# A loads-and-sums move: W_out fetched and its column sums taken in the SSM stage, and the second head pair's weight copy placed behind the first half-unit's copies

## The reference, cut to what matters

```python
xn = layernorm(x)
s = L0_attn(xn)          # 16 heads of 128, elu(q)+1 and elu(k)+1, causal linear attention, @ Wo.T
g = silu(L0_ffn(xn))     # 8 experts, top 2, and a shared one
x = x + s * g
xn = layernorm(x)
zxbca = xn @ W_in.T      # L1_attn: x, z, b, c of 32 heads x 64, and a
decay = exp(-exp(a))
states = states * decay + x_t * b_t      # a scan over 1024 tokens, per head a 64x64 state
y = (states @ c_t + x_t * D) * silu(z)
y = (y - mean(y)) * rsqrt(var(y) + 1e-5) * gamma + beta    # over 2048
s = y @ W_out.T
g = silu(L1_ffn(xn))     # int weights: (wq - 128) * scale; gate, up, down, 704 wide
x = x + s * g
```

## Time and profile before

| | |
|---|---|
| times of three executions | 1805.13, 1802.15, 1801.72 us; median 1802.15 |
| the profiled execution | 1803.97 us |
| its span, first to last instruction | 1802.2 us |
| mean granted TensorE clock | 0.969 |
| busy: TensorE, DVE, ACT, POOL | 92%, 64%, 42%, 37% of the span |
| last phase of batch 0 and of batch 1 begins at | 432.9 us, 1334.1 us |
| first SSM projection of the two batches | 504.1 us, 1399.5 us |

### The profile page before, as it was taken

How to read it: one execution, slowest core, us unless ns; L and a number is a source line. 1 busy time by engine, 2 the same in 40 slices (tenths; PEclk the granted TensorE clock), 3 DMA queues, 4 the chain that set the end, 5 groups by cost and what they waited for, 6 DMA issues and landing times.

```text
span 1802.2 us, 29615 instructions
## 1 busy us (share of the span) xinstructions
PE 1652.1 (92%) x11068; PEld 1370.2 (76%) x11068; DVE 1153.2 (64%) x2041; ACT 758.6 (42%) x1379; POOL 664.2 (37%) x500
## 2 busy tenths in 40 slices
PE   5997899898979999999969978998989899999988
PEld 3886677796868888887938866777968788888878
DVE  4334788653857777777753347886535677777767
ACT  3333455333434444444534334553334344444445
POOL 1454444101114555444514534441012155444535
PEclk9999999999989999999979989999999999999999
DMA  2333000001224443441023320000012343343410
GB/s 76 103 103 117 18 36 1 1 1 56 71 85 127 126 133 118 129 140 49 13 70 103 108 111 19 36 1 1 1 56 71 96 139 118 122 140 126 132 33 25
DMA packets 60061, 135.68 MB, mean 75 GB/s; under 512 B 8128, under 2 KB 12736, under 8 KB 59408
## 3 DMA queue, kind: packets, MB, share of 16 engines
q1 hardware_dynamic: 59920, 133.79, 23.6%
HBM read 130.81 MB, written 2.95 MB: 74 GB/s over the span
## 4 chain that ended last, share of the span: by engine, by line
PE 65%; DVE 11%; POOL 7%; issue 6%; ACT 6%; DMA 2%; SPq 1%; POOLq 0%; DVEq 0%; ACTq 0%
PE ps L550 29%; PE ps L607 6%; PE ps L869 4%; PE ps L893 4%; PE ps L646 4%; PE ps L831 3%; POOL silu_g L450 3%; PE ps L905 3%; PE ps L586 3%; POOL rb L468 2%; POOL fw_lo L435 2%; PE ps L880 2%; PE ps L748 2%; PE ps L599 2%; PE ps L749 2%
## 5 line engine op out<-in xcount | busy, mean ns | idle before, releaser
L550 PE MATMUL ps<-xnT_hi,w_in_hi 128*128 128x512 f32 x512 | 222.3, 434 | 0.0
L550 PE MATMUL ps<-xnT_lo,w_in_hi 128*128 128x512 f32 x512 | 203.0, 396 | 0.0
L550 PE MATMUL ps<-xnT_hi,w_in_lo 128*128 128x512 f32 x512 | 201.9, 394 | 0.0
L468 POOL TENSOR_TENSOR rb<-ra,rb 128x512 f32<-128x512 f32 x80 | 117.6, 1469 | 202.9 <-DVE rb L1532 202.9
L426 POOL TENSOR_TENSOR w_in_lo<-w_raw,w_in_hi 128x1024 fp32r<-128x1024 f32 x32 | 84.2, 2631 | 272.0 <-ACT w_in_hi L951 272.0
L1653 DVE TENSOR_TENSOR_SCAN lmat<-dec,ident 128x512 f32<-128x512 f32 x128 | 165.4, 1331 | 0.0
L1342 DVE TENSOR_TENSOR hid<-ps,silu_g 128x512 f32<-128x512 f32 (+1 forms) x80 | 55.1, 689 | 163.6 <-POOL silu_g L450 106.0
L513 POOL TENSOR_TENSOR yt<-yg,sz 128x512 f32<-128x512 f32 x64 | 82.1, 1283 | 172.9 <-ACT sz L1262 165.9
L550 PE MATMUL ps<-xnT_hi,fw_hi 128*128 128x512 f32 x312 | 127.9, 410 | 17.5 <-DVE fw_lo L1360 9.8
L435 POOL TENSOR_TENSOR fw_lo<-fw_raw,fw_hi 128x512 fp32r<-128x512 f32 (+1 forms) x56 | 62.6, 1119 | 185.3 <-ACT fw_hi L981 134.7
L550 PE MATMUL ps<-xnT_hi,fw_lo 128*128 128x512 f32 x312 | 125.6, 403 | 0.0
(11 more groups left out here) (194 smaller groups left out, 4392.8 us busy)
## 6 DMA issues: line engine op xcount, KB each, us to landing
dec<-dec_dram SPq DMA_DIRECT2D x64, 512.0 KB, 4.0
w_raw<-in_w_in SPq DMA_DIRECT2D x32, 512.0 KB, 4.8
wdec<-dec_dram SPq DMA_DIRECT2D x128, 128.0 KB, 3.9
pdec<-dec_dram SPq DMA_DIRECT2D x128, 128.0 KB, 3.7
fw_raw<-in_fw SPq DMA_DIRECT2D x40, 384.0 KB, 3.2
w_raw<-in_w_qkv SPq DMA_DIRECT2D x8, 768.0 KB, 4.2
comb<-comb_dram SPq DMA_DIRECT2D x8, 512.0 KB, 3.7
w_out<-in_w_o SPq DMA_DIRECT2D x2, 2048.0 KB, 10.7
```

Source lines behind the costliest of these rows:

```text
L468: nc.gpsimd.tensor_tensor(rb[:, k], ra[:, k], rb[:, k], ALU.add).then_inc(a_rot.sem, 1)
L550: mm = nc.tensor.matmul(out, left(l, k), right(r, k), start=(j == 0), stop=(j == len(steps) - 1))
```

## The change

The load of W_out goes from the start of the last phase, ahead of the FFN1 weights 2 to 5, to the third head pair of the SSM, behind the issue of that pair's weights, and with it the wait on the barrier goes away (a wait on the last matmul of the attention's output projection stands in its place). The 32 affine sums of batch 0 go from FFN1's steps 3 to 10 (four in a step) to the SSM's half-units 10 to 25 (two in each, behind the masked scores). On ACT `ssm_prep` of the second pair goes into the first half-unit of the loop, behind `xtok_copy`, and the gate's silu is done as eight pieces of 128x256 behind `z_silu` of the first eight half-units, in both batches.

```diff
--- before.py
+++ after.py
@@ -52,6 +52,7 @@
 YSLOTS = 3
 STATES = NC - 1
 SUFFIX = 8
+AFFINE_FROM = 10
 SH = 32
 
 LN_EPS = 1e-5
@@ -347,9 +348,6 @@
                 sp.wait_ge(f_wdl.sem, f_wdl.done(n - 2))
                 sp.dma_start(fw_raw[:, k % 2, :], src).then_inc(fw_in[k % 2], 16)
 
-            def phase_over(b, phase):
-                sp.wait_ge(phase_end, 4 * (b * PHASES + phase + 1))
-
             for j in range(NC // 2):
                 sp.sem_inc(stored[j], 16)
             for dst, src in ((ident4, a["ident4"]), (causal, a["causal"]), (earlier, a["earlier"]),
@@ -381,8 +379,6 @@
                     weights(split_qkv(b, i, 0), a["w_qkv"][bass.ds(i, 1)].rearrange("g p c -> p (g c)"), KT * QKV)
                 for k in range(2):
                     ffn_weights(b, NF0 + k, a["fw1"][k].bitcast(F32))
-                phase_over(b, 3)
-                sp.dma_start(w_out[:], a["w_out"]).then_inc(w_out_in, 16)
                 for k in range(2, NF1):
                     ffn_weights(b, NF0 + k, a["fw1"][k].bitcast(F32))
 
@@ -395,6 +391,9 @@
                 for h in range(HP):
                     n = b * HP + h
                     weights(split_ssm(b, h), a["w_in"][h], KT * XZBC)
+                    if h == 2:
+                        sp.wait_ge(o_mm.sem, o_mm.done(b * NC + NC - 1))
+                        sp.dma_start(w_out[:], a["w_out"]).then_inc(w_out_in, 16)
                     for hf in range(2):
                         u = 2 * n + hf
                         toks = slice(hf * HALF, (hf + 1) * HALF)
@@ -1278,20 +1277,22 @@
                         return
                     b_copy(u + 1)
                     xtok_copy(u + 1)
-                    if hf == 0 and 1 <= h and h + 1 < HP:
+                    if hf == 0 and h + 1 < HP:
                         ssm_prep(h + 1, (h + 1) % 2)
                     c_copy(u + 1)
                     btok_copy(u + 1)
                     z_silu(u)
+                    if u < 2 * b * HP + NC:
+                        c = u - 2 * b * HP
+                        if c == 0:
+                            act.wait_ge(f_sum.sem, f_sum.done(2 * b + 1))
+                        nc.scalar.activation(gate[:, c, :], gate[:, c, :], ACT.Silu)
                 u0 = 2 * b * HP
                 x_copy(u0)
                 b_copy(u0)
                 c_copy(u0)
                 xtok_copy(u0)
                 btok_copy(u0)
-                ssm_prep(1, 1)
-                act.wait_ge(f_sum.sem, f_sum.done(2 * b + 1))
-                nc.scalar.activation(gate[:], gate[:], ACT.Silu)
                 for u in range(u0, u0 + 2 * HP):
                     ssm_unit(u)
 
@@ -1710,9 +1711,13 @@
                     add_skip(u)
                     decayed_scores(u + 1, 0)
                     decayed_scores(u + 1, 1)
+                    if b == 0 and 0 <= u - AFFINE_FROM < NT:
+                        affine_sums(u - AFFINE_FROM)
 
                 def affine_sums(t):
 
+                    if t == 0:
+                        dve.wait_ge(w_out_in, 16 * 2)
                     for x in range(2):
                         if t == 0:
                             ins = nc.vector.tensor_scalar(affine[:, x, :], w_out[:, t, :], gamma_beta[:, t, x:x + 1], None, ALU.mult)
@@ -1728,11 +1733,6 @@
                         weights_lo1(b, u // 2 + 1, u % 2)
                     if u == 1:
                         decay_prefix()
-                    if b == 0 and 3 <= u < 11:
-                        if u == 3:
-                            dve.wait_ge(w_out_in, 16 * 2)
-                        for t in range(2 * (u - 3), 2 * (u - 2)):
-                            affine_sums(t)
                     if u >= 2 * NF1 - 2:
                         decay_scan(u0, u - (2 * NF1 - 2))
                 for hf in range(2):
```

## The result

| kernel | median of the runs, us | lowest to highest | profiled execution | its span |
|---|---|---|---|---|
| before (5 runs) | 1802.72 | 1801.72 to 1805.19 | 1803.97 | 1802.2 |
| changed (5 runs) | 1782.24 | 1779.52 to 1785.17 | 1785.17 | 1783.4 |

The ratio is 0.989, 95% interval 0.9869 to 0.9911: 20 us less, between 16 and 24. The forecast of 1782.7 us holds, and so does its range.

What follows compares the result with a forecast made beforehand. TensorE, busy 1652.1 us, was taken as the bound, with holes in FFN1 and the SSM's start. 5.9 + 7.2 + 6.4 us, 19.4 from unrounded rows, off the 1802.15 median gave 1782.7 us; range 1780.5 to 1789.

Steps and rivals of the forecast that it cites:

- (a): FFN1, batch 0: without the affine sums the stretch falls from 71.20 to batch 1's 65.30 us, 5.9 us less.
- (b): SSM's start: xT no longer waits behind second pair's weights and gate; 17.4 us stretch, 7.2 and 6.4 us less.
- (c): SSM half-units on ACT: eight gate pieces hide in idle time behind sz, cost 0; uncovered, at most 4.8 us a batch.
- (d): SSM loop, batch 0: sum pairs on DVE are covered, slack 0.2 us, cost 0; upper bound 6 us in all.
- (e): SSM loads, both batches: the 2 MB load behind the third pair's weights delays nothing, cost 0, at most about 1 us.
- B: Rival, SSM loop: pairs behind even half-units cost TensorE up to 0.75 us each, 6 us in all, 1788.7; chance 0.08.
- C: Rival, third pair: its weights are slowed by the 2 MB load, 6.9 us a batch, 1796.5; chance 0.04.
- D: Rival, SSM's start: second pair's weights late in their new place, 0.5 to 2 us a batch, about 1785.5; chance 0.06.
- E: Rival, even half-units: both sums wait for a w_in_lo, 27.8 us over 8 half-units, slower at 1810.5; chance 0.02.
- F: Rival, FFN1 and SSM's start: the holes return elsewhere, time within 3.6 us of before; chance 0.01.

Runs made afterwards that it cites:

- e4_whole: Changed kernel with the gate's silu in one piece again, ahead of the loop, second pair's weights still in the loop: 1780.24 us.
- e5_even: Changed kernel with all four affine sums of two half-units behind the even one, where POOL is at work: 1805.98 us.
- e6_odd: Changed kernel with all four affine sums of two half-units behind the odd one, where POOL is idle: 1781.09 us.
- e7_ahead: Changed kernel with the W_out load issued ahead of the third pair's weights in place of behind them: 1794.49 us.
- e10_both: Changed kernel plus FFN1's second weight tile made before step one, decay products later, first pair's weights two steps earlier, first decay scans behind FFN1's last step: 1767.34 us.
- e11_late: e10_both with the decay prefix moved to FFN1's steps 4 to 6 and all affine sums behind odd half-units: 1763.43 us.

## Why the prediction was right, and where not

**(a) FFN1, 5.9 us: right.** The stretch fell to 64.60 us here and to 64.5 to 65.8 in the five other kernels that only move the sums, so 5.4 to 6.7 us. Batch 1 was a measured batch 0 without the sums.

**(b) SSM's start, 7.2 + 6.4 us to a stretch of 17.4: the mechanism was right, and the low clock mis-sized.** The stretch without holes is 17.17 us, and TensorE's work from the turn of x takes 7.24 or 7.25 us in every kernel without the hole, as in the loop and as the forecast took it: those 1.61 us of low clock did go. But both terms also took the first ten microseconds of the stretch to be at full speed, as they are in batch 1 of the kernel before. In the profiled run they were not: behind the 1.2 us hole at FFN1's end, which the forecast kept, TensorE was at half speed in both batches, and 5.85 and 4.89 us were gained. In 10 of 17 batches with that hole it stayed at full speed. The forecast priced the hole at its idle time and nothing for the clock; it is worth 1.2 us, and 1.5 to 3.0 more where the low clock comes.

**(c) Gate pieces, 0: right, and the pieces are not needed** (e4_whole).

**(d) Sums in the SSM, 0 with an upper bound of 6: 0.1 to 0.3 us.** (The rest of the 0.5 us is TensorE's own wait behind the late weight load.) The pair behind an even half-unit took 1.9 to 2.3 us (2.5 forecast), once 2.76. The forecast had the second sum waiting for yt, which is what happens. What it left out is that POOL's place is not fixed: a weight load for which ACT waits 1.5 us moves it, and then the slack of 0.2 us is used up. The Trainium skill's rule (SBUF — State Buffer, "Who interferes with whom") is borne out by e5_even against e6_odd, 1501 against 478 ns.

**(e) The 2 MB load, 0: right.** The weights ahead of it landed after 5.1 us, and no engine waited; W_out landed after 10.4.

**The rivals.** B showed in its mildest form, 0.3 us at most. C did not come, and e7_ahead shows that it was two lines away. D did not come: the slack is 1.2 us. E did not come; a loss of its size came only with four sums at the place, by waits for POOL's short instructions. F fell.

**The sum.** 19.4 us forecast, 20.5 by the medians, 16.5 by the stretches of one profiled pair. The close agreement of the medians (1782.7 forecast, 1782.24 measured) is partly luck: the untouched stages alone move a run by 2 to 3 us, and whether the low clock comes moves it by as much again. The profiled execution of the changed kernel, with the low clock in both batches, is the slowest of its five.

## What to carry to other kernels

An instruction that waits for a load must stand behind everything on its engine that is ready and that the busiest engine needs; ACT's part, which is no more than that, gave 12.7 of the 19.6 us. Side work of DVE goes where POOL is idle, and how far POOL's place can shift (by a late load) belongs to the slack. After an idle stretch has been removed, look at what idle time still stands ahead of the place: low clock may stand behind that one too, even where the old profile happened to show none.

## What the hardware showed that was not expected

In the stretches looked at here DVE and POOL alternated instruction by instruction, so what DVE paid depended on the number of its instructions and on the length of POOL's: 0.48 us sums became 1.50 beside POOL's of 1.3 to 1.5, and a copy of 32x8 took 2.21 us beside POOL's of 2.1 in e10_both (0.16 alone, in e11_late). DVE's instructions with an input in PSUM (mt, hid) were not held. A longer instruction paid one such wait, like a shorter one: fw_lo of 128x512 took 2.35 us and of 128x256 2.32 beside POOL's 2.1 us products, against 0.68 and 0.42 alone. One long sum in place of four short ones was not tried.

A hole of 1.2 us in TensorE's work was followed by half speed in 7 of 17 batches and not in the other 10, at the same length and place. At 1.5 to 3.0 us a batch it can make up much of the 5 us by which runs of this kernel differ.

A 512 KB load issued 0.6 us behind a 2 MB one (which landed after 9.7 us) landed 1.3 us after it, 10.4 us after its own issue; issued 0.6 us ahead of it, it landed after 5.1 us, near the 4.8 us that is the median of such loads in the loop.
